# A fused attention and low-rank FFN block on one core: scores ahead of the values' projection, the attention output in the scores' banks, and the input brought in already turned

## The reference

```
x = x + attn(layernorm(x));   x = x + ffn(layernorm(x))

attn(x):  xn = layernorm(x) * ln_g + ln_b;  q, k, v = split(xn @ W_qkv + b_qkv)
          gate = sigmoid(x @ W_gate + b_gate);  gate = gate / (mean(gate) + EPS)
          q = relu(q * gate)**2 + EPS;  k = relu(k * gate)**2 + EPS      (16 heads of 32)
          token by token:  kv += k (x) v;  ks += k;  out = (q . kv) / (q . ks + EPS)
          return out @ W_proj + b_proj
ffn(x):   gelu((x @ U1) @ V1 + b1) @ U2 @ V2 + b2                        (rank 128, 2048 wide)
```

## Time and profile before

| | us |
|---|---|
| median of 3 runs (lowest, highest) | 1758.83 (1758.03, 1759.03) |
| the profiled execution, its own time | 1757.7 |
| its span, first to last instruction | 1755.6 |
| PE busy | 1722.4 (98%) |
| PE weight loads busy | 1458.9 (83%) |
| DVE busy | 1385.1 (79%) |
| POOL busy | 825.7 (47%) |
| ACT busy | 676.4 (39%) |
| share of PE in the chain that ended last | 93% |

### The profile page before, as it was taken

How to read it: one execution, slowest core, us unless ns; L and a number is a source line. 1 busy time by engine, 2 the same in 40 slices (tenths; PEclk the granted TensorE clock), 3 DMA queues, 4 the chain that set the end, 5 groups by cost and what they waited for, 6 DMA issues and landing times.

```text
span 1755.6 us, 39773 instructions
## 1 busy us (share of the span) xinstructions
PE 1722.4 (98%) x16729; PEld 1458.9 (83%) x16729; DVE 1385.1 (79%) x2222; ACT 676.4 (39%) x1242; POOL 825.7 (47%) x1027
## 2 busy tenths in 40 slices
PE   7899999999999999999999999999999999999997
PEld 4688888888888888888888888888888888888876
DVE  7877878877878877787788788778788778878775
ACT  4243343443434333433433433434433434344332
POOL 3354445444545544544544554544454445455440
PEclk9999999999999999999999999999999999999999
DMA  6101010011010011010011010010100110100000
GB/s 212 35 19 37 26 37 26 26 37 37 26 37 25 26 37 37 26 37 26 25 37 32 31 28 29 31 37 26 37 25 26 37 38 25 37 25 26 31 20 25
DMA packets 34720, 61.41 MB, mean 35 GB/s; under 512 B 3864, under 2 KB 6448, under 8 KB 34544
## 3 DMA queue, kind: packets, MB, share of 16 engines
q1 hardware_dynamic: 33680, 57.31, 9.9%
q10 hardware_dynamic: 864, 1.57, 0.3%
HBM read 41.96 MB, written 16.91 MB: 34 GB/s over the span
## 4 chain that ended last, share of the span: by engine, by line
PE 93%; DVE 1%; ACT 0%; issue 0%; POOL 0%; DVEq 0%
PE wide L795 18%; PE wide L797 18%; PE wide L796 18%; PE wide L802 7%; PE ps_h L795 4%; PE wide L949 4%; PE wide L983 4%; PE ps_h L796 3%; PE ps_q L795 3%; PE ps_h L797 3%; PE ps_q L796 3%; PE ps_q L797 3%; PE wide L977 2%; PE ps_q L962 1%; PE ps_h L1004 1%; PE ps_h L1003 1%
## 5 line engine op out<-in xcount | busy, mean ns | idle before, releaser
L394 POOL TENSOR_TENSOR h_lo<-h_full,h_hi 128x512 fp32r<-128x512 f32 x244 | 314.5, 1289 | 418.9 <-DVE h_hi L620 418.9
L795 PE MATMUL wide<-wx_hi,zt_hi 128*128 128x512 f32 x1024 | 415.2, 405 | 4.4 <-DVE zt_lo L575 3.6
L797 PE MATMUL wide<-wx_hi,zt_lo 128*128 128x512 f32 x1024 | 405.7, 396 | 0.0
L796 PE MATMUL wide<-wx_lo,zt_hi 128*128 128x512 f32 x1024 | 405.1, 396 | 0.0
L475 ACT ACTIVATE h_full<-ps_h,cols 128x256 f32<-128x256 f32 x512 | 204.0, 474 | 128.5 <-PE ps_h L797 128.1
L797 PEld LDWEIGHTS wide<-wx_hi,zt_lo 128*128 128x128 f32 x1024 | 192.8, 188 | 46.3
L795 PEld LDWEIGHTS wide<-wx_hi,zt_hi 128*128 128x128 f32 x1024 | 193.6, 189 | 42.5 <-DVE zt_lo L575 4.4
L796 PEld LDWEIGHTS wide<-wx_lo,zt_hi 128*128 128x128 f32 x1024 | 193.5, 189 | 37.4 <-issue 0.7
L357 POOL TENSOR_TENSOR small<-moments,eps_col 128x1 f32<-128x1 f32 x128 | 25.8, 201 | 395.7 <-DVE moments L764 326.4
L620 DVE CAST h_hi<-h_full 128x512 fp32r<-128x512 f32 x256 | 163.9, 640 | 35.5 <-ACT h_full L475 33.9
L698 DVE TENSOR_TENSOR probs<-wide,causal 128x2048 f32<-128x2048 f32 x64 | 146.6, 2291 | 50.2 <-PE wide L949 50.2
(11 more groups left out here) (150 smaller groups left out, 3798.0 us busy)
## 6 DMA issues: line engine op xcount, KB each, us to landing
xs<-L_attn_x SPq DMA_DIRECT2D x64, 256.0 KB, 2.7
out<-x1s SPq DMA_DIRECT2D x64, 256.0 KB, 2.1
key_sums<-carry_rows SPq DMA_DIRECT2D x60, 256.0 KB, 3.1
x1s<-L_attn_W_gate SPq DMA_DIRECT2D x4, 256.0 KB, 4.1
x1s<-L_ffn_U SPq DMA_DIRECT2D x4, 256.0 KB, 3.3
carry_rows<-key_sums SPq DMA_DIRECT2D x64, 2.0 KB
probs<-L_attn_W_qkv SPq DMA_DIRECT2D x3, 256.0 KB, 5.7
bias<-L_attn_b_qkv ACTq DMA_DIRECT2D x3, 256.0 KB, 6.8
```

Source lines behind the costliest of these rows:

```text
L394: E.tensor_tensor(h_lo[:, i % SLOTS, :], h_full[:, i % SLOTS, :], h_hi[:, i % SLOTS, :].bitcast(F32), ALU.subtract).then_inc(s["h_lo_ready ...
L795: E.matmul(ps, wh, mh, start=start and i == 0, stop=False)
L796: E.matmul(ps, wh, ml, start=False, stop=False)
L797: mm = E.matmul(ps, wl, mh, start=False, stop=stop and i == last)
```

## The change

Four things change.

- **The input is also loaded turned.** The host passes a second copy, `x_turned`, with features on partitions. SP loads it into a new buffer `xt` (two chunks), writes each chunk's 128 means (one float per partition) to memory and reads them back as a row on all partitions (`rows`). POOL subtracts the row from `xt` in place (`center`). The scale (the reciprocal deviation) is applied later by DVE, when it takes the gate's projection out of PSUM; for keys, queries and values the scale was there already and has other terms now. `x_norm` and the transposes `tz` go away for all chunks but the first; `z_head` and `z_tail` read `xt` in SBUF instead of `ps_t` in PSUM. `small_stats` has five operations instead of six, and DVE takes the statistics of the chunk after next right after the values.
- **The scores go ahead of the values' projection**, with one `h_pair` in between; the state and the output follow the projection directly. The other `h_pair` come after the output, and the four `q_pair` come together at the end of the step.
- **The output is written into the scores' four banks** (`ps_t, ps_c, ps_d, ps_b`); the key sums go to `ps_b`, once `ot_lo` is done; P goes to `ps_h[1]`; `ps_a` is a bank of its own for KEY, VALUE and y.
- **POOL's list** has key_lo and `center` ahead of all four `h_tail`; DVE's has one `h_head` ahead of `ot_lo` and three behind `zt_lo`.

The core of the diff:

```diff
+        xt = sb("xt", [P, 2, KT, P])
+        rows = sb("rows", [P, 2, P])
...
-        ps_out = [ps_c, ps_d, ps_b, ps_a]
-        out_cols = wide[:, DM:5 * DM].rearrange("p (j n) -> p j n", j=HPG)[:, :, 0:P]
+        out_cols = scores[:, :].rearrange("p (j n) -> p j n", j=HPG)[:, :, 0:P]
+        ps_a = bank("ps_a")
...
+                    sp.dma_start(xt[:, c.half, :, :].rearrange(flat), x_turned[c.slot, c.row // P, :, :])\
+                        .then_inc(xt_in[c.slot], 16)
+
+            def means_out(c):
+                if c.exists:
+                    sp.wait_ge(s["x_stats"], c.done(2, 2))
+                    sp.dma_start(rows_dram[c.slot, :].rearrange("(t a) -> t a", a=1), small[:, c.slot, 2:3])\
+                        .then_inc(rows_out[c.slot], 16)
+
+            def means_in(c):
+                if c.exists:
+                    sp.wait_ge(rows_out[c.slot], c.turned())
+                    wait(sp, s["z_ready"], Chunk(c.p, c.off - 2).done())
+                    sp.dma_start(rows[:, c.half, :],
+                                 rows_dram[c.slot, :].rearrange("(a t) -> a t", a=1).broadcast_to([P, P]))\
+                        .then_inc(rows_in[c.slot], 16)
...
+            def center(c):
+
+                if not c.exists:
+                    return
+                mine = xt[:, c.half, :, :]
+                pool.wait_ge(xt_in[c.slot], c.turned())
+                pool.wait_ge(rows_in[c.slot], c.turned())
+                E.tensor_tensor(mine, mine, rows[:, c.half, :].unsqueeze(1).broadcast_to([P, KT, P]),
+                                ALU.subtract).then_inc(s["z_ready"], 1)
...
+                center(Chunk(p, b + 1))
                 if ffn.exists and not is_last(p):
+                    h_tail(ffn, pairs[0])
                     h_tail(ffn, pairs[1])
                     h_tail(ffn, pairs[2])
                     h_tail(ffn, pairs[3])
...
-            def x_norm(c):
...
-                    E.tensor_tensor(zt_lo[:, :, :].rearrange(flat), ps_t[:, :],
+                    turned = xt[:, c.half, :, :].rearrange(flat) if c.p or c.off else ps_t[:, :]
+                    E.tensor_tensor(zt_lo[:, :, :].rearrange(flat), turned,
                                     zt_hi[:, :, :].rearrange(flat).bitcast(F32), ALU.subtract)\
                         .then_inc(s["zt_ready"], 1)
...
-                    E.tensor_tensor(gate[:, :], ps_b[:, :], bias[:, GATE, :], ALU.add)\
+                    dve.wait_ge(s["x_small"], n.done(5, 2))
+                    E.scalar_tensor_tensor(out=gate[:, :], in0=ps_b[:, :], scalar=small[:, n.slot, 1:2],
+                                           in1=bias[:, GATE, :], op0=ALU.mult, op1=ALU.add)\
                         .then_inc(s["gate_evac"], 1)
...
-                tz(Chunk(p, b + 1))
+                if ffn.exists:
+                    if b % 2:
+                        h_pair(ffn, pairs[1])
+                    h_pair(ffn, pairs[2])
+                    if b % 2 == 0:
+                        h_pair(ffn, pairs[3])
+                if n.exists:
+
+                    if c.exists:
+                        pe.wait_ge(s["ot_ready"], c.done())
...
+                    E.matmul(ps_b[:, :], causal_r[:, :], key_hi[:, :], start=True, stop=False)
+                    E.matmul(ps_b[:, :], causal_r[:, :], key_lo[:, :], start=False, stop=True)\
+                        .then_inc(s["sums_done"], 1)
+                if ffn.exists and b % 2:
+                    h_pair(ffn, pairs[3])
```

235 lines of the change are left out of this document (106 added, 129 removed).

## The result

The kernel after takes **1751.3 us** (median of 6 runs, 1750.8 to 1753.7), the kernel before 1758.9 in the same comparison: a ratio of 0.9959, 95% interval 0.9946 to 0.9972: 0.4% faster, small but clear of the noise. The forecast was 1749.8. The profiled execution took 1750.9 instead of 1757.7, that is 6.8 less; the sum had said 9.0.

A forecast was written before the change was run, and what follows sets the result against it. TensorE, busy 600.00 of 600.00 us, bounds the kernel. Per pair of steps 0.80 removed less 0.66 new waits gives 4 us over 30 pairs; start 3, end 2: 1757.7 becomes 1748.7 profiled, median 1749.8; range 1735 to 1770.

The forecast's parts named there:

- Place 1: Key sums, every step: they wait for `ot_lo`; second matmul 0.11 us late, 0.22 per pair of steps.
- Place 2: Scores, even steps: they wait 0.16 us for ScalarE's `key_t`; bounds 0.07 and 0.35.
- Place 3: Last `q_pair`, even steps: waits 0.25 us for the fourth `h_tail`, with DVE and POOL alternating; bounds 0 and 0.6.
- The chain: DVE and POOL alternate from `h_tail` 0 through `zt_lo` and roundings; `h_tail` 3 ends 7.22 us after the output block.
- Place 4: First `h_pair` of odd steps: waits 0.03 us for `pt_lo`; bounds 0 and 0.15.
- The waits did not vanish: Rival: weights come in time, DVE and POOL fall into step, some 0.25 us per pair remain: 1737; chance 0.25.
- the turn that would have made 1772: Rival at last `q_pair`: DVE takes one more 0.55 us turn between tails; waits 1.41 per pair; chance 0.22.
- The means were not late: Rival: means out and back exceed a step, `center` holds up POOL's tails and TensorE: over 1800; chance 0.03.

The follow-up runs named there:

- the kernel with half a `q_pair` ahead: Kernel after with two roundings up, both hidden products ahead of the scores (even steps) and half the first `q_pair` ahead of the key sums: 1731.7 us.
- the kernel where POOL is idle: Kernel after with VectorE's rounding of the first hidden tile moved ahead of the values' evacuation: 1745.7 us.

## Why the prediction came out as it did

The direction and the first three places were right, and each of the three was taken away by an experiment of its own. The total missed by 1.5 us: the sum for the profiled execution by 2.2 (1748.7, measured 1750.9), and its distance to the median, 0.4 instead of 1.1, by 0.7 the other way.

**Where the gain is, and what of it is luck.** The sum had 4 us for the middle, 3 for the start and 2 for the end. In the two traces the key transposes of the fifth step start 2.3 us earlier (146.07 instead of 148.32), those of the last but one 3.4 earlier (1687.03 instead of 1690.39), and the span ends 6.5 earlier: 2.3 at the start, 1.1 in the middle, 3.1 at the end. The middle, which had the careful sum, gave about a quarter of what it had; the ends, which had rough estimates, gave nearly all. The middle's 0.03 per pair is the difference of 0.78 and 0.75: one more wait of 0.1 us in either step would have made it a loss. So that the total came within 1.5 us is in part luck.

**What the removal is worth.** The opening of the prediction, that what TensorE does not have to do is gained in full, is wrong already for the old order: there 0.12 of 0.80 came, since the next wait stood 0.22 us away. The price itself was good. 0.40 per step was read from what the next block shifts. In the new order it is 0.45 (0.36 and 0.09), but other changeovers are added (the values' projection now has the state, a block of small tiles, behind it, and takes 2.88 instead of 2.79), so that the order without waits, as in the kernel with half a `q_pair` ahead, has a pair of 52.40: 0.78 less than 53.18. The forecast had 0.80.

**Place 1**, the key sums: forecast 0.11 per step, measured 0.11 and 0.10. Right, and for the reason named: with work in between the 0.11 is gone, so it came with the wait, and in the row of weight loads above the load behind a wait starts together with its matmul, at 880.88.

**Place 2**, the scores: 0.16 forecast, 0.15 in the row, 0.13 when it was taken away.

**Place 3**, the last `q_pair`: 0.25 forecast, 0.34 to 0.36 measured. The chain was right to 0.01 us (7.21 for 7.22), and `zt_lo` took part in it. The Trainium skill's rule ("SBUF — State Buffer", section "Who interferes with whom") agrees with the trace: 0.88 for `zt_lo` while POOL subtracts, 0.68 in the kernel where POOL is idle, and 0.69 throughout for the PSUM reader. What was left out is the term that I had used two paragraphs earlier: a product behind a wait hasn't loaded its weights. That is 0.11 here too (0.23 instead of 0.12 to the second matmul). The wait itself was 0.24, against the forecast's 0.25.

**Place 4**, the first `h_pair` of odd steps: nothing is seen of it. In its place stands one that I had not listed, 0.06 at the fourth `h_pair` of odd steps, behind the activation of the second. I had asked of each moved block who releases it, but not of this one: its bank comes free with the activation of the tile two places ahead, and between the two lay the scores and a product in the old order (1.9 us), now a product and the key sums (1.2 to 1.3).

The waits make 0.22 + 0.13 + 0.36 + 0.06 = 0.77 one by one (0.75 together) where the forecast had 0.66. 0.78 - 0.75 = 0.03 per pair is 1 us; forecast 4. What was off in the sum is the term of place 3, by 0.10, and the missing 0.06; the 0.03 of place 4 went the other way.

**The ends.** In the start the masked scores' two waits of 2.4 are gone (output at 56.34 without a wait). Against them stand, in each of these two steps, 1.4 us at the key sums behind `ot_lo` (within the 0.5 to 1.4 that the prediction took) and 0.78 at the scores behind `key_t`, and one wait that I did not name: the second chunk's gate projection needs `ps_b`, which the key sums now use.

```profile
39.29 0.77 PE L822 MATMUL scores<-wx_hi,zt_hi 128*128 128x512 f32 x1 [4.28 <-DVE key_sums L762]
58.86 0.50 PE L1010 MATMUL scores<-key_hi,causal 128*128 128x512 f32 x1 [1.44 <-DVE ot_lo L747]
```

The projection started at 37.52 before. 2.3 gained in all, forecast 3. At the end it is 3.1, forecast 2. The wait of the earlier trace rows did shrink, from 1.79 to 0.38:

```profile
1724.30 0.66 PE L829 MATMUL scores<-ident,zs 128*128 128x128 f32 x4 [0.38 <-DVE zs L803]
```

But TensorE's granted clock has a part in both ends, and the prediction left it out. In the closing step it falls to half, the lower of its two levels, after TensorE has waited for the second layer norm (2.37 us before, 2.25 and then 1.41 after); before, then after, with the columns of the earlier trace rows:

```profile
1710.00:1717.00 7.00, 4.91 (x24) 4.29 (x28) 1.70 (x4) 2.12 (x5) 1.31 (x2) 0.54 0.00 0
```

```profile
1709.90:1713.30 3.40, 3.40 (x40) 2.95 (x39) 0.57 (x1) 1.24 (x3) 0.00 (x0) 0.50 0.00 0
```

The kernel before spends some 3 us more at half the clock there; the last key transposes, for one, take 0.77 us in it and 0.41 after. My estimate from these two stretches is that this is worth at most 1.5 us of the 3.1. At the start it is the other way round: between 20 and 60 us the granted clock was 0.96 before and 0.91 after. With one trace of each kernel it can't be told what of this belongs to the change.

**The rivals.** The waits did not vanish, and the tails did not take the turn that would have made 1772: on odd steps no `q_pair` waits. The means were not late, though their write takes 7.8 us where the prediction had leaned on DMAs that land in 3.1. The Trainium skill ("DMA: Bandwidth & Descriptors", table of specifications) says that such small pieces are written by read-modify-write; the trace fits with it but doesn't show the mechanism.

## What to carry to other kernels

Work that is taken from the bounding engine may have been the cover of another engine's result: before pricing its removal, ask of the next two waits behind it how much slack they had with it in place (here `ot_lo`, 0.22 us ahead of `y`, so that 0.37 of 0.41 came back). A chain of two engines that alternate is shortened only where it begins; moving the first member ahead gave 0.20 of 0.36, since the second still waited for a rounding further back. And each hoist has a size: a third of a microsecond of cover paid, twice as much pushed a GpSimd operation into a VectorE product that it had cleared by 0.44 us. No wait shows such a distance beforehand; one has to compare the times of the two engines' operations. Last, take the middle and the ends of a run apart before believing a total: here the middle gave 1 us of 6.8.

## What the runs showed of the hardware that I had not expected

A write of 128 pieces of 4 bytes from 128 partitions lands after 7.1 to 11.2 us (median 7.8), while the 256 KB tiles of `x_turned` take 4.2. A VectorE operation that GpSimd held up ends a good while behind it: `zt_lo` and the key's product 0.55, a rounding 0.28. The matmul after one that waited starts 0.11 us late, whether the wait itself was 0.01 (the key sums) or 0.24 (the last `q_pair`); behind a set of transposes it is 0.09, without any wait. And TensorE's busy share did not see waits of 0.1 to 0.2 us at all: the kernel before without its transposes was busy for 599.1 of 600 us while it gave back 0.28 in every step.
